# Mean squares as two rounded products, with their squares split over two engines, and the values of the fourth tile ahead of them

## What is computed

```python
xn = layernorm(x)
q = (q0 @ fq1.T + b1) * (q0 @ fq2.T + b2)      # q0, k0, v: projections of xn, 16 heads of 16
k = (k0 @ fk1.T + b3) * (k0 @ fk2.T + b4)
# causal linear attention in chunks of 64:
o = qc @ cumsum_before(kc.T @ vc) + tril(qc @ kc.T) @ vc
o = o * rsqrt(mean(o * o, over the 16 numbers of a head) + 1e-5) * norm_w     # the head norm
attn = o @ wo.T
# mixture of 8 experts, chosen by cumulated probability (top-p 0.9):
probs = softmax(xn @ router_w.T); w = probs where kept, else 0
ffn = sum over e of w[:, e] * (silu(xn @ gate[e].T) * (xn @ up[e].T)) @ down[e].T
out = x + attn + ffn
```

## Time and profile before

| | |
|---|---|
| median of 3 runs | 837.93 us (837.58 to 839.29) |
| profiled execution | 839.02 us, of which its span, first to last instruction, is 837.3 us |
| mean granted TensorE clock | 0.970 |
| PE busy | 753.8 us, 90% |
| DVE busy | 496.0 us, 59% |
| ACT busy | 389.6 us, 47% |
| POOL busy | 321.6 us, 38% |
| chain that ended last, by engine | PE 48%, issue 16%, DVE 14%, DMA 10%, POOL 5%, ACT 4% |

### The profile page before, as it was taken

The page is one execution under the profiler, slowest core; times in us unless marked ns, Lnnn a source line. Parts: engine busy times, 40 slices in busy tenths (PEclk is TensorE's granted clock), DMA queues, the critical chain, the costliest instruction groups (busy, mean ns, idle before and its releaser), DMA issues.

```text
span 837.3 us, 19531 instructions
## 1 busy us (share of the span) xinstructions
PE 753.8 (90%) x6592; PEld 675.8 (81%) x6593; DVE 496.0 (59%) x1162; ACT 389.6 (47%) x909; POOL 321.6 (38%) x358
## 2 busy tenths in 40 slices
PE   5899999999999998249999989999999999899993
PEld 4677676767777776249999989999999999899993
DVE  5667786868685948325464564654555645645642
ACT  3435354444445352325464454554554545545642
POOL 2000000010101031225565656666666656666663
PEclk9999999999999998659999999999999999999997
DMA  2320302112030211414344353353354353533332
GB/s 85 119 77 2 101 12 89 49 52 92 9 101 0 76 14 53 112 40 122 55 93 99 57 131 63 52 133 61 60 126 63 55 135 53 133 58 60 57 59 36
DMA packets 42785, 59.54 MB, mean 71 GB/s; under 512 B 8336, under 2 KB 38032, under 8 KB 41616
## 3 DMA queue, kind: packets, MB, share of 16 engines
q0 software_dynamic: 19776, 27.16, 20.0%
q1 hardware_dynamic: 22992, 32.16, 11.7%
HBM read 37.15 MB, written 22.15 MB: 71 GB/s over the span
## 4 chain that ended last, share of the span: by engine, by line
PE 48%; issue 16%; DVE 14%; DMA 10%; POOL 5%; ACT 4%; POOLq 2%; DVEq 0%; ACTq 0%
PE A L1068 9%; PE A L1069 8%; PE A L1070 8%; DMA xg<-gather_table,g_idx 6%; PE O L1070 3%; PE O L1068 3%; PE O L1069 3%; PE S L1108 3%; DVE s_sb L763 3%; DMA out<-ybuf,s_idx 3%; POOL out L461 2%; PE A L1299 2%; POOL xg L447 2%; PE S L1070 2%; PE S L1069 2%
## 5 line engine op out<-in xcount | busy, mean ns | idle before, releaser
L461 POOL DMA_INDIRECT out<-ybuf,s_idx x98 | 159.8, 1631 | 62.5 <-POOL s_idx L457 46.7
L1068 PE MATMUL A<-gT_hi,w_hi 128*128 128x256 f32 x588 | 166.2, 283 | 6.3 <-issue 4.8
L1069 PE MATMUL A<-gT_lo,w_hi 128*128 128x256 f32 x588 | 165.2, 281 | 0.0
L1070 PE MATMUL A<-gT_hi,w_lo 128*128 128x256 f32 x588 | 165.2, 281 | 0.0
L447 POOL DMA_INDIRECT xg<-gather_table,g_idx x100 | 101.7, 1017 | 109.0 <-ACT w_tok L661 55.5
L365 POOL TENSOR_TENSOR on_lo<-on,on_hi 128x512 fp32r<-128x512 f32 x16 | 20.4, 1276 | 303.7 <-ACT on_hi L517 303.7
L1068 PEld LDWEIGHTS A<-gT_hi,w_hi 128*128 128x128 f32 x588 | 112.9, 192 | 8.1 <-issue 8.1
L1042 DVE TENSOR_TENSOR h_lo<-h,h_hi 128x256 fp32r<-128x256 f32 x196 | 82.9, 423 | 59.6 <-ACT h_hi L689 59.6
L1068 PE MATMUL O<-w_hi,h_hi 128*128 128x256 f32 x392 | 114.4, 292 | 0.0
L1069 PEld LDWEIGHTS A<-gT_lo,w_hi 128*128 128x128 f32 x588 | 111.7, 190 | 0.0
L1070 PEld LDWEIGHTS A<-gT_hi,w_lo 128*128 128x128 f32 x588 | 111.6, 190 | 0.0
(11 more groups left out here) (182 smaller groups left out, 1571.2 us busy)
## 6 DMA issues: line engine op xcount, KB each, us to landing
w_raw<-wffn SPq DMA_DIRECT2D x9, 1536.0 KB, 7.1
xa<-x SPq DMA_DIRECT2D x8, 512.0 KB, 6.0
gather_table<-xna SPq DMA_DIRECT2D x8, 512.0 KB, 4.5
xr<-x SPq DMA_DIRECT2D x8, 512.0 KB, 5.7
out<-yout SPq DMA_DIRECT2D x8, 512.0 KB, 3.0
out<-ybuf,s_idx POOLq DMA_INDIRECT x104, 3.8
xg<-gather_table,g_idx POOLq DMA_INDIRECT x100
w_raw<-wqk_nat SPq DMA_DIRECT2D x1, 512.0 KB, 4.8
```

Source lines behind the costliest of these rows:

```text
L461: pool.indirect_dma_start(out=out, out_offset=bass.IndirectOffsetOnAxis(ap=s_idx[:, sub:sub + 1], axis=0), in_=ybuf[:, sub, :], in_offset= ...
L1068: mm(out_ap, l_hi, r_hi, start=(k == 0), stop=False)
L1069: mm(out_ap, l_hi, r_lo, start=False, stop=False)
L1070: return mm(out_ap, l_lo, r_hi, start=False, stop=(k == n - 1))
```

## The change

- `head_mean` becomes an fp32r tile, and the mean squares become two products of fp32r tiles: `head_mean` with the high part of the squares, and with their low part.
- ScalarE squares `O[half]` twice: rounded into `on_hi` (which lies idle then), and in f32 into `sq`. GpSimd subtracts the one from the other into `on_lo` (`squares_low`). The products wait for GpSimd (`sqlo_ok`) instead of ScalarE. For half 0, ScalarE waits before the squares until the output projection has read `on_hi`.
- On TensorE, values and logits of tile 3 move ahead of the mean squares, those of tile 1 behind the transposes and scores 1, together with the wait for the logarithm. ScalarE copies tile 3's values before `head_rstd`, and the transposed keys before `heads_hi`. VectorE makes `masked_scores` 1 before the logits of tiles 1 and 3.
- On GpSimd, `squares_low` stands before each `outputs_low`; at the end, the one of block 7's half 1 stands behind `add_zeros(1)`.

The two lists of semaphore names, which gain `sqlo_ok`, are left out of the diff.

```diff
--- before.py
+++ after.py
@@ -112,7 +112,7 @@
 
         ident = sb("ident", [P, P])
         head_mask = sb("head_mask", [P, HH, DK])
-        head_mean = sb("head_mean", [P, P])
+        head_mean = sb("head_mean", [P, P], F32R)
         causal = sb("causal", [P, P])
         before = sb("before", [P, P], BF16)
         ones_bf = sb("ones_bf", [P, P], BF16)
@@ -359,6 +359,12 @@
             g.memset(vz[:, :, :, :, :], 0.0).then_inc(counts, 1)
             g.memset(yout[:, 0, 0:1], 0.0).then_inc(yout_free, DMA)
 
+            def squares_low(s, half):
+
+                pool.wait_ge(sq_ok, 2 * s + half + 1)
+                g.tensor_tensor(on_lo[:, half, :], sq[:, half, :], on_hi[:, half, :].bitcast(F32),
+                                ALU.subtract).then_inc(sqlo_ok, 1)
+
             def outputs_low(s, half):
 
                 pool.wait_ge(onhi_ok, 2 * s + half + 1)
@@ -394,11 +400,13 @@
 
             def first_half(s, first, last):
                 if not first:
+                    squares_low(s - 1, 1)
                     outputs_low(s - 1, 1)
                 if last:
                     add_zeros(0)
 
             def second_half(s, last):
+                squares_low(s, 0)
                 outputs_low(s, 0)
 
             first_half(0, True, False)
@@ -409,6 +417,7 @@
             first_half(NBLK - 1, False, True)
             second_half(NBLK - 1, True)
             add_zeros(1)
+            squares_low(NBLK - 1, 1)
             outputs_low(NBLK - 1, 1)
             add_zeros(2)
 
@@ -566,7 +575,7 @@
                 a.activation(w_hi[par][:, bass.ds(c0, PW)], w_raw[:, bass.ds(c0, PW)], ACT.Copy).then_inc(whi_ok, 1)
 
             def values_out(s, t):
-                act.wait_ge(v_ps, TT * s + (1, 3, 2, 4)[t])
+                act.wait_ge(v_ps, TT * s + (1, 4, 2, 3)[t])
                 a.activation(vz[:, t, :, 0:4:3, :], values_banks[t][:, 0:D].rearrange("p (g e d) -> p g e d", e=2, d=DK),
                              ACT.Copy).then_inc(v_ok, 1)
 
@@ -575,8 +584,12 @@
                 a.activation(k_tok[:, half, :, :].rearrange("p b m -> p (b m)"), kt_banks[half][:, 0:2 * P],
                              ACT.Copy).then_inc(kt_ok, 1)
 
-            def squares(s, half):
+            def squares(s, half, first=False):
+
                 act.wait_ge(pv_ps, 4 * s + 2 * (half + 1))
+                if half == 0 and not first:
+                    act.wait_ge(wo_ps, 2 * s)
+                a.activation(on_hi[:, half, :], O[half][:, :], ACT.Square)
                 a.activation(sq[:, half, :], O[half][:, :], ACT.Square).then_inc(sq_ok, 1)
 
             def first_half(s, first, last):
@@ -584,12 +597,13 @@
                     squares(s - 1, 1)
                 values_out(s, 0)
                 values_out(s, 2)
+                values_out(s, 3)
                 if not first:
                     head_rstd(s - 1, 1)
+                keys_by_token(s, 0)
+                if not first:
                     heads_hi(s - 1, 1)
                 values_out(s, 1)
-                values_out(s, 3)
-                keys_by_token(s, 0)
                 act.wait_ge(ls_ok, s + 1)
                 a.activation(ex[:, :, :], ls[:, :, :], ACT.Exp).then_inc(ex_ok, 1)
                 if not last:
@@ -602,7 +616,7 @@
                 if not last:
                     norm_apply(s + 1)
                 keys_by_token(s, 1)
-                squares(s, 0)
+                squares(s, 0, first)
 
             def second_half(s, last):
                 if not last:
@@ -878,8 +892,8 @@
                 if not first:
                     one_hot(s - 1, 1)
                     head_norm(s - 1, 1, chain)
+                masked_scores(s, 1)
                 logits_out(s, 1)
-                masked_scores(s, 1)
                 softmax_head(s, chain)
                 if not last:
                     norm_stats(s + 1, chain)
@@ -1137,8 +1151,9 @@
                 last.then_inc(pv_ps, 1)
 
             def mean_squares(s, half):
-                pe.wait_ge(sq_ok, 2 * s + half + 1)
-                mm(ms_bank[:, :], head_mean[:, :], sq[:, half, :], start=True, stop=True).then_inc(ms_ps, 1)
+                pe.wait_ge(sqlo_ok, 2 * s + half + 1)
+                mm(ms_bank[:, :], head_mean[:, :], on_hi[:, half, :], start=True, stop=False)
+                mm(ms_bank[:, :], head_mean[:, :], on_lo[:, half, :], start=False, stop=True).then_inc(ms_ps, 1)
 
             def slot_tokens(s):
 
@@ -1193,14 +1208,15 @@
                 values_logits(s, 2)
                 pe.wait_ge(qk_ok, 4 * s + 2)
                 scores(s, 0, first)
+                values_logits(s, 3)
                 if not first:
                     mean_squares(s - 1, 1)
-                    pe.wait_ge(ln_o_ok, 2 * s)
-                values_logits(s, 1)
-                values_logits(s, 3)
                 pe.wait_ge(lg_ok, 2 * s + 1)
                 keys_by_token(s, 0)
                 scores(s, 1)
+                if not first:
+                    pe.wait_ge(ln_o_ok, 2 * s)
+                values_logits(s, 1)
                 project(q_banks[1][0], 0, 1)
                 pe.wait_ge(lg_ok, 2 * s + 2)
                 project(q_banks[1][1], 1, 1).then_inc(proj_ps, 1)
```

More of the change, by code:

```diff
@@ L245, in build @@
                  "gathered xg_free ghi_ok glo_ok gu_ps silu_ok h_free hhi_ok hlo_ok y_ps ya_ok yd_ok "
-                 "wt_ok scattered_a scattered_b pool_gate dve_gate pe_gate act_gate whi_ok")
+                 "wt_ok scattered_a scattered_b pool_gate dve_gate pe_gate act_gate whi_ok sqlo_ok")
         sems = {n: sem(n) for n in names.split()}
@@ L253, in build @@
          gathered, xg_free, ghi_ok, glo_ok, gu_ps, silu_ok, h_free, hhi_ok, hlo_ok, y_ps, ya_ok, yd_ok,
-         wt_ok, scattered_a, scattered_b, pool_gate, dve_gate, pe_gate, act_gate, whi_ok) = [sems[n] for n in names.split()]
+         wt_ok, scattered_a, scattered_b, pool_gate, dve_gate, pe_gate, act_gate, whi_ok, sqlo_ok) = [sems[n] for n in names.split()]
         nat = w_raw[:, 0:2 * KC * D].rearrange("p (m c k) -> p m c k", m=2, c=KC)
```

## The result

The kernel after takes 844.74 us, median of 20 executions; the kernel before, on the same chip, 839.85 of 20. The ratio is 1.0054, with a 95% interval of 1.0036 to 1.0072: slower by 0.5%, and 844.74 lies 4 us above the predicted range. One of the 20 executions of after took 4106 us and is left out of the ratio; the median of the other 19 is 844.57. The profiled execution of after took 847.81, its span is 846.1.

A forecast was written before the change was run, and what follows sets the result against it. Bound in blocks 1 to 6: TensorE and VectorE in series. Gains 2.0 (six blocks) and 0.95 (last block), losses 0.3 (first block) and 3.4 (end): net 0.75 lost, 838.7 us against the median, 839.8 against the profiled execution; range 834.9 to 840.7.

The forecast's parts named there:

- the turn of a block: Steps from half 1's squares to the next softmax: product ends 0.73 later, projection 1.03 earlier, net gain 0.33 us per block.
- the exclusion: At the softmax: GpSimd's low outputs hold VectorE's `ls` through a shared port, cutting the gain from 0.80 to 0.33 per block.
- (a): Rival at the softmax: `ls` runs beside GpSimd unheld, 4.8 us gained in six blocks, 835.9 us; chance 0.33.
- (b): Rival before half 1's mean squares: TensorE's new wait is longer, `on` 0.3 later, gain gone, 840.5 us; chance 0.12.
- The last block: Block 7, where VectorE waits for TensorE: TensorE's 1.03 us less about 0.1 for the logits, so 0.95 gained.
- the end: Last mean squares: GpSimd's subtraction queues behind two indirect DMAs, all that follows 3.4 us later, bounds 1.9 to 4.9.
- the upper bound: Last mean squares and output projection: 4.9 us lost if the clock stays at its lower level and GpSimd starts late.
- edits with no price: Half 0's mean squares shorten by about 0.4 us, TensorE's wait for the mask grows, and nothing is lost.
- rival (c): Rival at half 0's lengthened TensorE stand, about 1.1 us: lower clock in each block, 14 us, about 853; chance 0.03.
- block 0: First block, without mean squares: six products moved behind scores 1 follow 0.27 us later, counted as 0.3 lost.

The follow-up runs named there:

- e3: Kernel after, with GpSimd's low outputs of half 1 held until the softmax's subtraction (`ls`) is done: 842.22 us, ratio 1.0028.
- e5: Kernel before with only the new order of work, keeping the single f32 product and one square: 839.87 us, ratio 0.9982.
- e8: Kernel before with the new order and GpSimd's low outputs of half 1 held until `ls` is done, no new arithmetic: 834.86 us, ratio 0.9949.
- e6: Kernel after, last subtraction ahead of the DMAs, low outputs held until `ls` is done, half 0 back to one f32 product and one square: 837.91 us, ratio 0.9967.
- e11: Kernel after, unchanged, profiled once more: 843.97 us.
- e1: Kernel after, with GpSimd's last subtraction (block 7, half 1) ahead of the second pair of indirect DMAs: 840.15 us, ratio 1.0010.
- e2: Kernel after, with an unneeded f32 product of the squares added ahead of half 0's rounded pair: 840.55 us, ratio 1.0022.
- e9: Kernel before with the new order in blocks 1 to 7 only and low outputs held until `ls` is done, block 0 in old order: 831.85 us, ratio 0.9897.
- e12: Kernel after, last subtraction ahead of the DMAs, low outputs held until `ls`, filler product in half 0, block 0 in old order: 833.93 us, ratio 0.9943.
- e4: Kernel after, last subtraction ahead of the DMAs, low outputs held until `ls` is done, filler product in half 0: 834.19 us, ratio 0.9952.
- e10: Kernel before, unchanged, profiled once more: 837.42 us.
- e7: Kernel after's arithmetic (two squares, GpSimd's subtraction, rounded pair) in the order of the kernel before: 866.16 us, ratio 1.0293.

## Why the prediction was wrong

**Right: the turn of a block.** Every time shown for the turn came out within 0.15 us, the exclusion with its direction and its size (e3), and the period 38.74 against 38.9. Rivals (a) and (b) are both out: `ls` is held, and TensorE waits 0.16 for GpSimd, where the forecast had 0.4 and (b) more than 0.6. The last block is an exception: 0.95 was counted and 0.48 gained, since the hold of the `ls` before it was left out. Five times 0.15 more in the other blocks made up for that. The gain is the order's: the projection no longer stands behind the wait for the logarithm. The product itself gains nothing (e5, e8 against e6).

**Right but for its size: the end.** Predicted 3.4, measured 4.1 and 4.5, within the bounds 1.9 to 4.9. The place was right: the subtraction stood behind two DMA instructions, and the pair ended 3.15 later. The rest is the output projection, which ran at the lower clock throughout, as the upper bound had it.

**Wrong: "edits with no price", the step on the half whose product gets shorter.** It found that "the wait grows" and took that as free, since TensorE is not the bound there. The wait of 1.13 us is indeed free; what follows it is not. The clock falls behind it in one to four blocks of an execution (three, one, four and two in after, e11, e1 and e3), for 1.54 us each. e2 shows it from the other side: fill the wait, and the lower clock and its cost are gone. This is rival (c), at the place where the prediction put it, but with two faults. It was given 0.03, since a stand of 2.08 was followed by the lower clock and one of 1.56 was not the earlier trace rows; one instance of each was too little to call 1.1 safe. And it was priced as all or nothing, 14 us in every block; a case of "some blocks, 1.5 to 6 us" was missing, so the range had no room for it. Its price came from twelve products of one block at the lower clock, when a stretch holds eight.

**Wrong: block 0.** Counted at 0.3 us lost, by the products moved behind the wait. That time is not lost: without a low stretch at 27 us the time from the first scores to the `ls` of block 1 is 0.6 shorter than before. With one it is 3.5 to 3.8 longer, and this was so in five of the nine profiled executions with the new order in block 0, though one of them, e2, had one stretch only and lost 1.0. In the medians the old order in block 0 is worth 3.0 without the new arithmetic (e9 against e8) and 0.3 with it (e12 against e4). The prediction had priced the moved products and not asked what the clock does in a block that already had two long stands.

The sum, with measured terms of the two pairs: blocks 2 to 7 -2.9 where -2.6 was predicted, the clock in them +1.5 and +4.6, the start to the `ls` of block 1 +4.8 and +4.5 where 0 was predicted, the end +4.1 and +4.5, behind it -1.8 and -1.1. That is 8.8 and 6.6 for the profiled executions. Both pairs had the slow case of block 0, which not every execution has; between the medians it is 4.9.

**What stays open.** What in block 0's new order lets the stretches grow from 3.4 to 6.8 us; stands of 1.57 us ahead of the first scores and 2.08 later are there in both orders, and in executions with and without the stretch. Why the clock falls in some repetitions of the same wait and not in others.

## What to carry to other kernels

A wait that grows off the critical path is not free on TensorE: ask of each edit that shortens or delays TensorE's work how long it then stands, and price a fall of the clock behind it per occurrence, with a chance, not as all or nothing. Before adding engines to a relay, try the reordering alone; here it held the whole gain, and the cheaper product only added a wait, a place in GpSimd's queue and a shorter cover. Give the first and last turn of a loop their own order and their own place in each queue: the last cost more than the six turns between them gained, and so did the first in the executions in which the lower clock came. And profile more than one execution before a stretch at the lower clock is put down to an edit: four of the nine with the new block 0 had none there.

## What the runs showed of the hardware

- The stand ahead of the second scores of half 0 is 1.02 to 1.14 us in blocks 1 to 6 of after, e11, e1 and e3, and in 10 of these 24 turns the lower clock followed, each time for 3.4 us at 1.2 GHz and 1.54 us of the block's time. In the same place it is 0.55 to 0.74 in before, e10, e5, e6, e8 and e9 and 0.15 to 0.28 in e2, e4 and e12: in none of these 54 turns did the clock fall. With stands of 1.06 and 0.78 in the other half as well (e7) it fell in every block, for up to 10.2 us.
- A small VectorE subtraction with both inputs in SBUF is held by a GpSimd subtraction that runs on SBUF, and the record shows it as a longer instruction (0.55 for 0.19), with no idle time before it. One semaphore wait on GpSimd, which stands idle for 4.71 us there, gives 0.34 us per block back (e3).
- An indirect DMA instruction holds GpSimd's queue for 1.6 us (1.57 and 1.64 in after). Two in a row, 339.17 to 342.69, made a subtraction behind them end 3.1 us later after the last `ls` than in e1, where it stands ahead of them (32.46 and 29.37).
- A product that nobody needs can shorten a kernel: e2, one f32 product of 512 columns more per block, is 4.2 us faster than after by the medians.
